# Channels 128 to 191 as pairs of 64-row matmuls, with |y| split once where it is stored

## The reference

```python
xs = jnp.einsum('bhwc,dc->bhwd', x, W1) + b1      # x is 16 x 64 x 64 x 768, W1 is 192 x 768
xs = jax.nn.gelu(xs, approximate=False)
xs = fft_low(xs)                                  # low-pass over h and w (a 32 x 32 mask), then abs
xs = jnp.einsum('bhwd,cd->bhwc', xs, W2) + b2     # W2 is 768 x 192
return x + xs                                     # all in float32
```

## Time and profile before

| | before |
|---|---|
| time, median of 3 runs | 2202.89 us (2202.61 to 2204.13) |
| profiled execution, its own time | 2201.8 us |
| its span, first to last instruction | 2200.0 us |
| PE busy | 2142.0 us, 97% |
| weight loads (PEld) busy | 1939.0 us, 88% |
| DVE, ACT, POOL busy | 1623.7, 1114.4, 327.5 us |
| DMA queue, share of 16 engines | 86.1% |

### The profile page before, as it was taken

How to read it: one execution, slowest core, us unless ns; L and a number is a source line. 1 busy time by engine, 2 the same in 40 slices (tenths; PEclk the granted TensorE clock), 3 DMA queues, 4 the chain that set the end, 5 groups by cost and what they waited for, 6 DMA issues and landing times.

```text
span 2200.0 us, 37824 instructions
## 1 busy us (share of the span) xinstructions
PE 2142.0 (97%) x12512; PEld 1939.0 (88%) x12512; DVE 1623.7 (74%) x2380; ACT 1114.4 (51%) x1861; POOL 327.5 (15%) x500
## 2 busy tenths in 40 slices
PE   6899999999999999999999999999999999999998
PEld 5799988989899898988989889998898989989876
DVE  6768687686877868778686776868768687786846
ACT  4565454645445555454554546545464544555532
POOL 1311111111111111111111111111111111111100
PEclk9999999999999999999999999999999999999999
DMA  6789988898888988988889888998889889888878
GB/s 209 234 304 350 347 316 306 322 361 335 302 325 322 345 322 314 344 317 329 333 319 350 316 320 318 351 344 314 305 322 363 332 293 334 325 342 324 317 291 344
DMA packets 253758, 707.40 MB, mean 322 GB/s; under 512 B 84242, under 2 KB 150930, under 8 KB 249620
## 3 DMA queue, kind: packets, MB, share of 16 engines
q1 hardware_dynamic: 253716, 706.86, 86.1%
HBM read 455.12 MB, written 251.66 MB: 321 GB/s over the span
## 4 chain that ended last, share of the span: by engine, by line
PE 92%; ACT 3%; DVE 2%; issue 1%; DMA 1%; SPq 0%; DVEq 0%; ACTq 0%
PE ps_h L277 24%; PE ps_h L278 11%; PE ps_o L341 8%; PE ps_o L338 8%; PE ps_o L335 8%; PE ps_o L332 8%; PE ps_o L331 8%; PE ps_o L316 8%; PE ps_f L288 2%; PE ps_o L310 2%; PE ps_f L290 2%; PE ps_f L289 2%; DVE xlo L464 1%; ACT xhi L372 1%; DMA rows_b<-filt 1%
## 5 line engine op out<-in xcount | busy, mean ns | idle before, releaser
L277 PE MATMUL ps_h<-w1s,xhi 128*128 128x384 f32 x3072 | 899.7, 361 | 25.0 <-DVE xlo L464 24.3
L278 PE MATMUL ps_h<-w1s,xlo 128*128 128x192 f32 x3072 | 770.9, 251 | 0.0
L277 PEld LDWEIGHTS ps_h<-w1s,xhi 128*128 128x128 f32 x3072 | 579.2, 189 | 42.5 <-DVE xlo L464 17.7
L511 DVE TENSOR_TENSOR xo<-ps_o,xo 128x1024 f32<-128x1024 f32 x384 | 470.3, 1225 | 178.5 <-PE ps_o L341 174.5
L278 PEld LDWEIGHTS ps_h<-w1s,xlo 128*128 128x128 f32 x3072 | 588.7, 192 | 7.6
L390 ACT ACTIVATE filt<-ps_f 128x384 f32<-128x384 f32 x256 | 126.2, 493 | 799.6 <-PE ps_f L290 799.2
L464 DVE TENSOR_TENSOR xlo<-xin,xhi 128x1536 fp32r<-128x1536 f32 x256 | 450.4, 1759 | 3.9 <-ACT xhi L372 3.9
L575 POOL TENSOR_TENSOR diff<-hid 128x192 f32<-128x192 f32 x240 | 166.8, 695 | 1462.6 <-ACT hid L381 1460.6
L372 ACT ACTIVATE xhi<-xin 128x1536 fp32r<-128x1536 f32 x256 | 377.8, 1476 | 8.2 <-DMA xin<-xt_dram 7.9
L473 DVE TENSOR_TENSOR hid<-ps_h,b_rows 128x192 f32<-128x192 f32 x512 | 181.0, 354 | 185.4 <-PE ps_h L278 183.1
L341 PE MATMUL ps_o<-ob,w2b_hi 128*128 128x512 f32 x768 | 303.4, 395 | 1.0 <-DVE ob L502 1.0
(11 more groups left out here) (52 smaller groups left out, 2056.6 us busy)
## 6 DMA issues: line engine op xcount, KB each, us to landing
xin<-xt_dram SPq DMA_DIRECT2D x256, 768.0 KB, 7.3
xo<-xt_dram SPq DMA_DIRECT2D x128, 1536.0 KB, 12.2
out_dram<-xo SPq DMA_DIRECT2D x128, 1536.0 KB, 8.6
rows_a<-filt SPq DMA_DIRECT2D x256, 128.0 KB, 5.2
cols_a<-rows_a SPq DMA_DIRECT2D x64, 512.0 KB, 3.7
rows_b<-filt SPq DMA_DIRECT2D x256, 64.0 KB, 6.2
cols_b<-rows_b SPq DMA_DIRECT2D x64, 256.0 KB, 4.2
xo<-w1t_dram SPq DMA_DIRECT2D x1, 576.0 KB, 4.5
```

What stands on the lines that cost most here:

```text
L277: nc.tensor.matmul(ps_h[tt][:, 0:2 * D], hi, w1s[:, k, :], start=k == 0, stop=False)
L278: ins = nc.tensor.matmul(ps_h[tt][:, D:2 * D], lo, w1s[:, k, 0:D], start=False, stop=k == KC - 1)
L511: nc.vector.tensor_tensor(x, ps_o[u % 2][:].rearrange("p (j a n) -> p j a n", j=2, a=2), x, ALU.add).then_inc(s_add, 1)
```

## The change

**Layout.** |y| is kept no longer as `ya` and `yb` but already split, as `ahi`, `alo` (128 channels) and `bhi`, `blo` (64 channels twice: image columns of even parity in rows 0 to 63, of odd parity in rows 64 to 127). The banks and the corner constants are reordered to fit. **Output units.** A unit is now one block of 128 output channels and 1024 tokens, two PSUM banks `o[0]` and `o[1]` for the two parities. Its six whole products are as before; channels 128 to 191 are three pairs of matmuls with 64 contraction rows, rows 0 to 63 into one bank and rows 64 to 127 into the other. Built, these carry a tile size of 64 x 128 at row 0 and row 64, all others 128 x 128 (the corner sums 128 x 32, before and after). Units of even number do whole products first, those of odd number last. **Split.** ACT stores |y| into `yabs` and copies the high part from there; DVE subtracts the low part, once per bank. `split_hi` and `split_lo` of the token groups are gone. **Bias.** It is added by DVE with the residual (`scalar_tensor_tensor`). **DMAs.** Residual and result move per unit, 512 KB with 4096 contiguous bytes per partition, 12 slots.

```diff
@@ PE
-                for jj in range(2):
-                    nc.tensor.matmul(o, w2a_hi[:, c], oa_hi[:, r, :], start=True, stop=False)
-                    nc.tensor.matmul(o, w2a_lo[:, c], oa_hi[:, r, :], start=False, stop=False)
-                    nc.tensor.matmul(o, w2b_lo[:, c], ob1[:, r, :], start=False, stop=False)
-                    nc.tensor.matmul(o, w2a_hi[:, c], oa_lo[:, r, :], start=False, stop=False)
-                    ins = nc.tensor.matmul(o, w2b_hi[:, c], ob[:, r, :], start=False, stop=True)
+                    for w, y in ((w2a_hi, ahi), (w2a_lo, ahi), (w2a_hi, alo)):
+                        for v in range(2):
+                            ins = nc.tensor.matmul(o[v], w[:, c], y[:, v, n], ...)
+                    for w, y in ((w2b_hi, bhi), (w2b_lo, bhi), (w2b_hi, blo)):
+                        for v in range(2):
+                            r = slice(v * DB, (v + 1) * DB)
+                            ins = nc.tensor.matmul(o[v], w[r, c], y[r, n], ...)
+                if u % 2 == 0:
+                    whole(True)
+                    halves(False).then_inc(s_o, 1)
+                else:
+                    halves(True)
+                    whole(False).then_inc(s_o, 1)
@@ ACT, y_bank
-                nc.scalar.activation(slot, bank(b).rearrange("p (m n) -> p n m", m=4), ACT.Abs).then_inc(s_yev, 1)
+                if b >= YBANKS or later(i):
+                    act.wait_ge(s_ylo, BANKS * i + b - YBANKS + 1)
+                y = yabs[:, b % YBANKS, :, :]
+                nc.scalar.activation(y, bank(b).rearrange("p (m n) -> p n m", m=4), ACT.Abs).then_inc(s_yev, 1)
+                act.wait_ge(s_yev, BANKS * i + b + 1)
+                nc.scalar.activation(y_slot((ahi, bhi), b), y, ACT.Copy).then_inc(s_yhi, 1)
@@ DVE
+            def y_lo(i, b):
+                dve.wait_ge(s_yhi, BANKS * i + b + 1)
+                nc.vector.tensor_tensor(y_slot((alo, blo), b), yabs[:, b % YBANKS, :, :],
+                                        y_slot((ahi, bhi), b).bitcast(F32), ALU.subtract).then_inc(s_ylo, 1)
@@ DVE, add_unit
-                nc.vector.tensor_tensor(x, ps_o[u % 2][:].rearrange("p (j a n) -> p j a n", j=2, a=2), x, ALU.add).then_inc(s_add, 1)
+                nc.vector.scalar_tensor_tensor(x, ps_o[u % 2][:], b2_cols[:, k:k + 1], x, ALU.add, ALU.add).then_inc(s_add, 1)
@@ SP, one turn
+                        for u in units_at(s - 1):
+                            store(i - 1, u)
+                        for u in units_at(s + FIRST_O):
+                            load_xo(i - 1, u)
```

More of the change, by code:

```diff
@@ L141, in later, with y_slot @@
             return not isinstance(i, int) or i > 0
[L143 to L147, removed]
         def bank(b):
             return ps_o[b % OBANKS // 2][:, 512 * (b % 2):512 * (b % 2 + 1)]
[L152 to L157, removed]
+        def y_slot(part, b):
+            c, v = divmod(b, YBANKS)
+            a, o = part
+            whole = a[:, v, :] if v < 2 else o[:]
+            return whole.rearrange("p (n m) -> p n m", m=BCOLS)[:, :, BMULS * c:BMULS * (c + 1)]
         def units_at(s):
-            return [O_PER_STEP * (s - FIRST_O) + n for n in range(O_PER_STEP)] if s >= FIRST_O else []
+            return [O_PER_STEP * (s - FIRST_O) + n for n in range(O_PER_STEP)] if FIRST_O <= s < FIRST_O + UNITS // O_PER_STEP else []
         def turns(eng, head, turn):
@@ L252, in turn @@
                 if c:
[L253 to L258, removed]
+                    for u in units_at(STEPS - 1):
+                        store(i - 1, u)
             turns(sp, head, turn)
             for n in range(XO_SLOTS):
-                sp.wait_ge(s_out[n], 16 * 2 * IMAGES)
+                sp.wait_ge(s_out[n], 16 * (UNITS // XO_SLOTS) * IMAGES)
         @block.tensor
@@ L309, in filter_h_chunk @@
                     y = bank(b)
-                    nc.tensor.matmul(y, corner[:, P:2 * P] if v == 2 else corner[:, 0:P], corner_hw[:, v // 2, :], start=True, stop=False)
+                    nc.tensor.matmul(y, corner[:, P:2 * P] if v == 2 else corner[:, 0:P], corner_hw[:, v % 2, :], start=True, stop=False)
                     for m in range(4):
                         if v < 2:
-                            data = cols_a[:, CHUNK * c + 4 * v + m, :]
+                            data = cols_a[:, CHUNK * c + 2 * m + v, :]
                         else:
@@ L342, in out_unit, with whole @@
-                ins.then_inc(s_o, 1)
+                o = [bank(2 * (u % 2) + v) for v in range(2)]
+                def whole(first):
+                    for w, y in ((w2a_hi, ahi), (w2a_lo, ahi), (w2a_hi, alo)):
+                        for v in range(2):
+                            ins = nc.tensor.matmul(o[v], w[:, c], y[:, v, n], start=first and w is w2a_hi and y is ahi,
+                                                   stop=not first and w is w2a_hi and y is alo)
+                    return ins
@@ new lines, in halves @@
+                def halves(first):
+                    for w, y in ((w2b_hi, bhi), (w2b_lo, bhi), (w2b_hi, blo)):
+                        for v in range(2):
+                            r = slice(v * DB, (v + 1) * DB)
+                            ins = nc.tensor.matmul(o[v], w[r, c], y[r, n], start=first and w is w2b_hi and y is bhi,
+                                                   stop=not first and w is w2b_hi and y is blo)
+                    return ins
+                if u % 2 == 0:
[4 more added lines that the diff above has]
+                    whole(False).then_inc(s_o, 1)
@@ L551, in turn @@
                         hid_tile(here[0], 2 * here[1] + 1)
-                    if c and (g := split_at(s)) is not None:
-                        split_lo(i - 1, g)
                     if units:
@@ L557, in turn @@
                         hid_lo_pair(*here)
+                    if c and s < CHUNKS:
+                        for v in range(YBANKS):
+                            y_lo(i - 1, YBANKS * s + v)
                     if a and s == STEPS - 1:
@@ L609, in filters @@
         for w2 in range(2):
-            for first, b, w in ((0, 0, m), (0, 1, 2 * m), (64, 1, 2 * m + 1)):
-                terms = (-sin * sin[w], sin * cos[w], cos * sin[w], -cos * cos[w])
+            for first, b, w in ((0, 0, 2 * m), (64, 0, 2 * m + 1), (0, 1, 2 * m + 1)):
+                terms = (-sin * sin[w % 4], sin * cos[w % 4], cos * sin[w % 4], -cos * cos[w % 4])
                 for j, term in enumerate(terms):
```

149 lines of the change are left out of this document (43 added, 106 removed).

## The result

The changed kernel takes **2252.6 us** (median of 4 runs, 2246.0 to 2256.7), the kernel before 2202.8 us beside it (2201.6 to 2204.1). The ratio is 1.0225, 95% interval 1.0213 to 1.0238: slower by 49.8 us. The time lies inside the predicted range and on the likelier side, but 38 us above the 2215 us forecast: the loss is four times the 12 us that were expected.

A forecast was written before the change was run, and what follows sets the result against it. PE was taken as the bound, without gaps in filter steps (7.30 us) and output steps (8.60 us). Terms −90 + 90 + 15 − 3.5 = +12 on 2201.8 gave 2213.5, forecast as 2215 us; range 2140 to 2290.

The forecast's parts named there:

- Matmuls, −90: Output steps: 18 times 0.233 us instead of 20, with pairs side by side; −0.467 us a step, −90 us.
- serial pairs: Rival for output steps: the two 64-row matmuls of a pair don't overlap; 2460 us, chance 0.09.
- Change of tile size, +90: Output steps: two changes of 0.18 us plus 0.11 us for the second half-array's later start; 0.47 us a step, +90 us.
- x: Extra time of an output step's 64-row run, taken as 0.47 us; break-even at 0.41.
- The lag of 0.11 us inside the run: 64-row run of output steps: the second half-array gets its first weights 0.11 us later and stays behind; 21 us.
- the rival that rests on such starts: Output steps: both of a pair start together, changes cost 0.36 us; 2193 us, within a 0.11 case shared with cheap changes.
- The rival that the array does not empty: Output steps: row tiles don't empty the array, only 0.11 us a step remains; 2145 us, chance 0.25.
- The stage, +15: Filter steps: storing and splitting |y| on ACT makes its loop 8.29 us, delaying the first output unit; +15 us.
- DVE, DMAs, 0: DVE's changed work is covered and the smaller residual and result transfers cost nothing; up to 15 us if DMA runs full.
- Ends: Last turn: earlier output start about −1 us, shorter last store −2.5 us; together −3.5 us.
- I am wrong above all if the change of tile size is not what it is around the corner sums: Warning sign for output steps: the 0.18 us a change was read from the corner sums' 128 x 32 tile.

The follow-up runs named there:

- The longer body: The kernel before, with 96 already satisfied waits a turn added to PE's steps inside the loop: 2256.4 us, ratio 1.0238.
- the runs with waits ahead: The kernel before, with 32, 64 or 128 satisfied waits on PE once ahead of its loop: 2247.0, 2239.4 and 2299.8 us.
- the one with 75: The changed kernel, whole and with its loop, with 75 satisfied waits on PE once ahead of the loop: 2201.5 us, ratio 0.9993.
- run 18: Not a follow-up run: "run" is a verb here, and output steps take 18 paces of 0.233 us each.
- without the jump: The changed kernel with PE's loop over images written out, nothing else: 2194.6 us against 2201.7 of the kernel before, ratio 0.9966.
- the run with four changes: The changed kernel, PE's loop written out, all units whole products first, so tile size changes four times a step: 2270.6 us, 1.0313.
- the late copies: The changed kernel, PE's loop written out, high-part copies of filter steps made one step later except the last step's: 2163.2 us, 0.9822.

## Why the prediction was off

**The step that failed.** The sum, "−90 + 90 + 15 − 3.5 = +12", has no term for PE's jump back. The forecast counted four more matmuls a step and took them as free beyond their pace; it never asked what PE's *list* has to fit into. This term is 49.8 us lost with the loop and 7.1 gained without it, each against the kernel before on its own chip: **+57 us**, in 12 jumps 4.8 us each, 3.2 us of gap and about 1.6 of half clock. The longer body shows the length, the runs with waits ahead the place, and the one with 75 that nothing else is in it. That the gap is a fetch of instructions is read from q8: a packet in each gap, the first matmul 2.6 us after its start however long the gap, and none at the jumps of the kernels that have no gap. No record names the fetch as what PE waits for. Why some gaps bring half clock and others do not stays open. That 2252.6 us lies inside the range is luck: the range was made of other cases, of tile size and overlap, and none of them is what happened.

The Trainium skill, "Runtime: NRT & Kernel Launch", section "Instruction fetch mechanics", says that PE's buffer holds 2048 instructions, is refilled in blocks of 256, and that a jump to an instruction outside the window waits for the fetch. The 16 KB packets of 256 instructions and the gaps agree; the runs fit seven blocks that stay, 1792 instructions and not 2048. The same section of the Trainium skill speaks of a window of two pages around a branch; here the kernel before jumps back over a body of 1673 instructions without a gap, so for PE two are too few, and the measurement decides. I had not drawn on that page.

**Matmuls, −90**: right. Output steps run 18 paces of 0.233 us and the changes; the run with both members in the same rows excludes serial pairs.

**Change of tile size, +90**: mechanism right, size off. x is 0.39 us (0.387) and not 0.47, so +74 us. The two changes cost 0.19 and 0.20 us (0.18 read from the corner sums), though a row tile is another tile. The lag of 0.11 us inside the run is not there: the members of a pair start 3 to 4 ns apart in the records. What the Trainium skill, "TensorE: Matmul & The Clock Gate", section "Measured speedup vs the span model", has for row tiles, about 4 ns, agrees, and the rival that rests on such starts was the closest to what happens: it said 2193 us, and without the jump the kernel has 2194.6. So the two changes measured 0.39 us where 0.36 was reckoned, and the 21 us of the lag were not there. The rival that the array does not empty is excluded by the run with four changes.

**The stage, +15**: right. Step 4 and the filter steps together are 1.0 us longer in the trace without the jump (40.28 against 39.39 us, and the part of step 4 that is output 0.08 shorter), in 15 turns; the late copies show that it can be had back, and with it the 1.2 us that the earlier trace rows show before the first output unit.

**DVE, DMAs, 0**: right. The add came out 0.06 us longer and is hidden: in output steps DVE waits for PE. The last low part, the one that the first output unit needs, takes the 0.69 us that were reckoned; the 60 of 1.1 us come earlier in their steps. The smaller DMAs left no wait on PE.

**Ends**: the last turn −3.9 (−3.5 forecast), the first 18 pairs −3.2 (taken as nothing; no run shows why).

The sum as measured: −90 + 74 + 15 − 3.9 − 3.2 = −8 us, against −7.1 measured without the jump (2194.6 against 2201.7); with +57 it is +49, against +49.8. My "I am wrong above all if the change of tile size is not what it is around the corner sums" named the wrong place: that price held, and the break came from outside the steps.

## What to carry to other kernels

Before adding instructions inside or ahead of a hardware loop, count the instructions of the engine that sets the end: a body that just fitted can stop fitting, and then each round pays a gap at the jump and may pay slow matmuls behind it. The sign in a profile is idle put to "issue" at the same place every round, with a packet of the instruction queue in each such gap; many packets alone are no sign. Writing the loop out, or shifting it, tells in one run whether that is the cause. Weigh the change itself with that out of the way: here 0.3% of gain stood behind 2.3% of loss, and 1.8% once, with the loop written out, the stage's new work was moved to where its engine waits.

## What the runs showed of the hardware

- With PE's loop in place, 32 satisfied waits ahead of it cost 2.0% (1.4 to 2.6), though they run once. All runs fit a body that must lie within seven blocks of 256 instructions; the rule is reckoned from the nine kernels that keep the loop, and seen only on PE.
- A jump back that misses moves a 16 KB packet, 256 instructions, and the first matmul starts 2.57 to 2.69 us after the start of that packet in all 12 gaps of the changed kernel.
- Around 10 of these 12 gaps of 2.5 to 4.1 us the granted clock was 1.2 GHz for 3.4 or 6.8 us, beginning between 1.0 us before the gap's end and 1.5 us after it, also while PE was fully busy; at 64 instructions ahead, gaps of 1.9 to 2.6 us brought it in two of 12.
- A DVE subtraction of 128x512 took 0.69 us, and 1.08 to 1.10 in the 60 cases in which an addition of GpSimd ran beside it.
- Two 64-row products from different rows, into different PSUM banks, take 0.233 us together, as long as one of 128 rows; from the same rows 0.466.
- A change between 128-row and 64-row tiles costs 0.19 to 0.20 us each way: 0.09 before the first matmul of the new size, read as the array emptying, and 0.10 to 0.11 before the second, read as weights loaded in the open.
